# First routing of a mixture-of-experts layer: gates, dummy products and the first silu product reordered

## The chip, the cores and the metric

One core of one Trainium2 chip. The metric is the device time in microseconds of one execution, as the median of several runs. A core has TensorE (PE, matrix products), VectorE (DVE), ScalarE (ACT), GpSimd (POOL) and SyncE (SP), each with its own instruction queue worked off in order; semaphores order them against each other. Here SyncE issues the plain DMAs and the DMA transpositions, GpSimd the gathers and scatters by index.

## The reference

```python
# x [2, 1024, 256], ctx [2, 77, 256], mask [2, 1024, 77]
def xattn(q, k, v, mask, Wq, Wk, Wv, Wo, bo):        # 16 heads of 64
    dots = where(mask, -max, heads(q @ Wq) . heads(k @ Wk) * 64 ** -0.5)
    return merge(softmax(dots) . heads(v @ Wv)) @ Wo + bo
def ffn(x):                                           # 9 experts of 704, top 2
    scores = sigmoid(x @ gate.T + bias)
    top, selected = top_k(scores, 2); top = top / (sum(top) + 1e-20)
    for e in range(9):
        h = silu(x @ w1[e].T) * (x @ w3[e].T)
        out += weight_of(e) * (h @ w2[e].T)
x = x + xattn(layernorm(x), ctx, ctx, mask, ...)
x = x + ffn(layernorm(x), ...)
```

## The kernel before

**Attention.** The 2048 tokens are 16 tiles of 128 (NT = 16), worked in a software pipeline `step(n)` written out by hand for each engine. For tile n TensorE makes the scores; with lags of 2 to 5 steps it turns the probabilities (`prob_turn`), multiplies them by the folded value and output weights (`project`), VectorE adds the residual (`residual`), takes mean and variance (`stats`, `aggregate`), GpSimd the inverse root (`rstd`), VectorE or ScalarE the second layer norm (`normalise2`), TensorE transposes this in fp32 (`gate_turn`), ScalarE copies it (`gate_copy`), TensorE multiplies by the gate (`gate_logits`), VectorE adds the bias (`logits`) and finds the two best experts (`pick`). SyncE stores the normed rows (`store_xn2`), from which GpSimd gathers later.

**Routing in two parts.** The tokens of the first 11 tiles (K1 = 11) are routed first, in the `drain()` between attention and experts, and fill the first 14 expert tiles (NF1). VectorE makes one-hot tables (`experts_of`), TensorE counts (`ranks`), VectorE computes each token's slot (`first_slots`) and the two halves of a one-hot map (`first_rows`, L1323, `v1_ok`), TensorE multiplies them into a list of token ids (`first_ids`, 22 products of 14 columns), VectorE writes the list (`first_index`, `idx_ok`), and GpSimd starts the gathers. `ids_of(0)` gives the expert number of each tile. The rest is routed between the expert tiles.

**Experts.** 40 tiles of 128 gathered tokens (NF). For tile t: GpSimd `gather(t)`, ScalarE and VectorE split it into fp16 high and low parts (`fx_high`, `fx_low`), SyncE transposes by DMA (`turn_tokens`), except tile 0, which TensorE transposes itself (`first_turn`, then `first_high` and `first_low`). TensorE `up(t)`: four groups of six products, the first two for silu, the other two for the factor; ScalarE `silu`, VectorE `hidden`, ScalarE `h_high`, VectorE `h_low`, SyncE transposes by DMA (`turn_hidden`), TensorE `down(t)` with lag 2, ScalarE `weigh`, GpSimd `scatter`. `between(s)` runs in the middle of `up(s)`, behind its second group. Each engine walks the same `fstep(n)`, n from -3.

**Weights.** Expert weights come as 36 chunks of 544 KB through three buffers: SyncE `load_w(c)`, ScalarE `w_high` or `w_direct`, then the low half by GpSimd (`w_low`, up to chunk 30) or VectorE (`w_rest`, chunks 31 to 35). Each low half raises `w_lo_ok` by one, and the load into a buffer waits for the chunk that was in it (L418: `at_least(sp, w_lo_ok, c - SLOTS + 1)`, with SLOTS = 3). At the end of its drain SyncE has, in this order: store_x1(14), store_xn2(13), load_w(34), load_w(35); the first entry of fstep that moves data is turn_tokens(1) at n = -1.

**Dummy products.** `warm(n, bank)` issues n products of 128 x 128 ones into an unused bank. The drain has three places: WARM_IDS ahead of first_ids, WARM_OUT ahead of project(15), WARM_X0 ahead of first_turn.

**Order in the drain.** TensorE, from prob_turn(15): gate_turn(12), WARM_IDS, first_ids, gate_logits(12), WARM_OUT, project(15) with gate_turn(13) ahead of its chunk 4 and WARM_X0, first_turn ahead of chunk 9, then gate_logits(13). VectorE, from experts_of(0): sums(15), residual(13), p_low(14), stats(13), aggregate(13), first_slots, logits(11), first_rows, residual(14), first_index, p_low(15), ids_of(0), normalise2(13), logits(12), stats(14), aggregate(14), w_rest(31), w_rest(32), first_low, logits(13); then in fstep fx_low(1), residual(15), stats, aggregate, normalise2(14); fx_low(2), normalise2(15), shares(0), hidden(0), first_values, logits(14), pick(11). The helper `link` makes VectorE wait for its own last result.

Of the kernel before, what the change touches and what calls it, by code (L numbers as in the profile page):

```python
# [21 lines left out]
ALU = mybir.AluOpType  # L22
# [3 lines left out]
P = 128  # L26
# [11 lines left out]
E9 = 9  # L38
# [32 lines left out]
def build(nc, x, ctxT, mask, wq, wk, wv, wo, bo, wt, gate, gbias, consts, out):  # L71
    with ExitStack() as ctx:
# [221 lines left out]
        W_PRE = 4  # L294
        WARM, WARM_IDS, WARM_OUT, WARM_X0 = 30, 30, 16, 10

# [222 lines left out]
        def _(pe):  # L519
# [118 lines left out]
            def project(i):  # L638
                b = i // TPB
                at_least(pe, x1_ok, i)  # L640
                for c in range(NCH):
                    if i == NT - 1 and c == G_AT:
                        gate_turn(NT - 3)
                    if i == NT - 1 and c == X0_AT:
                        warm(WARM_X0, WARM_LATE)
                        first_turn()
                        eids[0] = expert(0)
                    if c % 4 == 0:
                        pe.wait_ge(pl_ok, 3 * i + c // 4 + 1)
                    for n, (lhs, rhs) in enumerate(((pt_h, b_hi), (pt_l, b_hi), (pt_h, b_lo))):  # L650
                        mm = pe.matmul(ps[:, 6, 0:D], lhs[:, c, :], rhs[:, b, c, :],  # L651
                                       start=(c == 0 and n == 0), stop=(c == NCH - 1 and n == 2))
                mm.then_inc(out_mm, 1)
# [31 lines left out]
            def first_ids():  # L685

                for q in range(2 * K1):
                    pe.wait_ge(v1_ok, q // K1 + 1)
                    mm = pe.matmul(map_of(0)[0], vhot1[:, q, :], R["u1"][:, q // K1, q % K1, 0, :],
                                   start=(q == 0), stop=(q == 2 * K1 - 1))  # L690
# [74 lines left out]
            def drain():  # L765
# [6 lines left out]
                prob_turn(NT - 1)  # L772
                gate_turn(NT + 1 - LAG_G)
                pe.wait_ge(sub_ok, 3 * NT)
                warm(WARM_IDS, WARM_LATE)
                first_ids()
                gate_logits(NT + 1 - LAG_G)
                warm(WARM_OUT, WARM_LATE)
                project(NT - 1)
                gate_logits(NT - 3)  # L780

# [66 lines left out]
            def between(s):  # L848
                if s in (1, 2):
                    gate_logits(NT - 3 + s)  # L850
# [4 lines left out]
            for s in range(NF + 2):  # L855
# [7 lines left out]
                if s < 2:  # L863
                    gate_turn(NT - 2 + s)
                if s == 1:
                    first_weights()
                if s == 2:
                    pe.wait_ge(lg_ok, NT)
# [11 lines left out]
        def _(act):  # L880
# [158 lines left out]
            p_high(NT - 1)  # L1039
            gate_copy(NT + 1 - LAG_G)  # L1040
            sigmoids(0, K1)
            act.activation(mx[:, 0, 0:1], eps[:], ACT.Silu)
            gate_copy(NT - 3)
            first_high()

# [74 lines left out]
        def _(dve):  # L1120
# [142 lines left out]
            def experts_of(ph):  # L1263
# [5 lines left out]
                dve.wait_ge(top_ok, hi)  # L1269
                for k in range(2):  # L1270
                    ins = dve.tensor_tensor(oh[:, k], by_expert(con[:, C_IOTA:C_IOTA + E9], n),
                                            idx[:, k].unsqueeze(2).to_broadcast([P, n, E9]), ALU.is_equal)
                link(ins)
                dve.tensor_tensor(s16[:, 0:hi, :], r["oh"][:, 0, 0:hi], r["oh"][:, 1, 0:hi], ALU.add).then_inc(s16_ok, 1)
# [175 lines left out]
            def drain():  # L1450
# [7 lines left out]
                p_low(NT - 2)  # L1458
                stats(NT - 3)
                aggregate(NT - 3)  # L1460
                first_slots()
                logits(NT - LAG_G)
                first_rows()
                residual(NT - 2)
                first_index()
                p_low(NT - 1)
                ids_of(0)
                normalise2(NT - 3)
                logits(NT + 1 - LAG_G)
                stats(NT - 2)  # L1470
                aggregate(NT - 2)
                w_rest(4 * EARLY + 3)
                w_rest(4 * E9 - 4)
                first_low()
                logits(NT - 3)

# [64 lines left out]
            def fstep(n):  # L1541
                if n == T_END + 1:
                    for g in range(2):
                        end_low(g)
                    return
                if onf(n, 1):
                    h_low(n - 1)
                if onf(n, -2) and n > -2:
                    fx_low(n + 2)
                if n == -1:  # L1550
                    residual(NT - 1)
                    stats(NT - 1)
                    aggregate(NT - 1)
                    normalise2(NT - 2)
                if n == 0:
                    normalise2(NT - 1)
                    shares(0)
                if n == 1:
                    held_of(0)
                if n == 2:  # L1560
# [31 lines left out]
                if n == 12:  # L1592
                    tile_weights(1)
                if onf(n, 0):
                    hidden(n)
                if n == 0:
                    first_values()
                    logits(NT - 2)
                    pick(NT - LAG_G)
                if n == 1:  # L1600
                    pick(NT + 1 - LAG_G)
# [14 lines left out]
        def _(pool):  # L1616
# [49 lines left out]
            def step(n):  # L1666
# [15 lines left out]
                if n == NT - 1:  # L1682
                    w_low(4 * EARLY + 2)
                if on(n, LAG_X1):
                    rstd(n - LAG_X1)
# [40 lines left out]
            def fstep(n):  # L1726
# [6 lines left out]
                if n + 3 == NF1:  # L1733
                    pool.wait_ge(idx_ok, 2)
                    stored(pool, NT - 2)
                    stored(pool, NT - 1)
                if n == -1:
                    rstd(NT - 2)
                if onf(n, -3):
# [59 lines left out]
```

## Time and profile before

| what | value |
|---|---|
| time, median of 3 runs | 423.49 us (422.23 to 424.11) |
| profiled execution | 422.82 us |
| its span | 421.0 us |
| PE busy | 403.9 us (96%), 3176 products |
| DVE, ACT, POOL busy | 275.2, 253.2, 246.9 us |
| L824, products of `up` | 960, 150.1 us |
| L844, products of `down` | 681, 80.8 us |
| mean granted clock of TensorE | 0.989 |

The span runs from the first to the last instruction of the execution; the time has 1.82 us more around it. Times of rows count from the span's start. The attention phase fills the span to about 170 us, the drain and the first expert tiles stand at 170 to 205, and the expert tiles follow to 412.

### The profile page before, as it was taken

The numbers are of one execution on the slowest core, as the hardware profiler recorded it, in microseconds if no ns is written. First come the engines' busy times: TensorE is split into PE (matmuls) and PEld (weight loads), VectorE is DVE, ScalarE is ACT, GpSimd is POOL, SyncE is SP. The second block draws the span as 40 slices with busy tenths as digits, with TensorE's granted clock in tenths as the row PEclk, the third lists the DMA queues.
The fourth block names the chain that finished last, engine by engine and source line by source line (L and its number), as shares of the span: only waits on it lengthen the run. The fifth ranks groups of instructions, "written<-read, shape, count | busy, mean of one in ns | idle before, by whom it ended". The sixth has DMA issues, their size and how long they took to land.

```text
span 421.0 us, 10140 instructions
## 1 busy us (share of the span) xinstructions
PE 403.9 (96%) x3176; PEld 307.2 (73%) x3176; DVE 275.2 (65%) x683; ACT 253.2 (60%) x444; POOL 246.9 (59%) x214
## 2 busy tenths in 40 slices
PE   8999999999999999789899999999999999999991
PEld 7777677778877877776677777777777777777781
DVE  1777989999899988987889854444444444444430
ACT  3759899999999986724655444444444444444430
POOL 6536789998999888253245534445444444444232
PEclk9999999999999999989999999999999999999997
DMA  7994456576575666256789978989889989989742
GB/s 228 342 321 132 132 160 201 161 189 201 155 235 166 177 187 190 74 151 120 154 138 139 146 131 133 141 139 129 150 141 142 141 139 140 143 134 153 119 68 36
DMA packets 106512, 66.03 MB, mean 157 GB/s; under 512 B 80992, under 2 KB 99808, under 8 KB 106464
## 3 DMA queue, kind: packets, MB, share of 16 engines
q1 hardware_dynamic: 98784, 54.90, 57.4%
q0 software_dynamic: 7680, 10.49, 16.5%
q8 instruction: 30, 0.49, 0.5%
q14 instruction: 18, 0.15, 0.1%
HBM read 36.23 MB, written 9.96 MB: 110 GB/s over the span
## 4 chain that ended last, share of the span: by engine, by line
PE 56%; issue 16%; DMA 14%; DVE 4%; POOLq 4%; POOL 3%; SPq 1%; ACT 0%; DVEq 0%
PE ps L824 12%; PE ps L621 12%; PE ps L651 11%; DMA out_rows<-work,idx_all 9%; PE ps L844 7%; PE ps L634 4%; POOLq L1709 3%; PE ps L558 3%; POOL work L1700 3%; PE ps L617 2%; DMA w_all<-in_wv 2%; PE ps L523 1%; DMA work<-work 1%; PE ps L667 1%; DMA work<-xn_rows,idx_all 1%
## 5 line engine op out<-in xcount | busy, mean ns | idle before, releaser
L824 PE MATMUL ps<-w_all,work 128*128 x960 | 150.1, 313 | 0.8 <-DVE work L1447 0.5
L824 PEld LDWEIGHTS ps<-w_all,work 128*128 128x128 f16 x960 | 93.6, 98 | 47.0 <-issue 1.2
L1721 POOL DMA_INDIRECT out_rows<-work,idx_all x40 | 64.2, 1606 | 102.5 <-ACT work L1076 101.1
L1516 DVE SCALAR_TENSOR_TENSOR work<-ps,work 128x352 f32<-128x352 f32 x80 | 41.2, 523 | 66.4 <-PE ps L824 66.3
L844 PE MATMUL ps<-w_all,work 128*128 x681 | 80.8, 273 | 1.1 <-DMA work<-work 1.1
L844 PEld LDWEIGHTS ps<-w_all,work 128*128 128x128 f16 x681 | 66.3, 98 | 12.0 <-issue 1.6
L1641 POOL TENSOR_TENSOR w_all<-stage,w_all 128x1088 f16<-128x1088 f32 x31 | 69.9, 2256 | 6.5 <-ACT w_all L916 6.2
L1055 ACT ACTIVATE work<-ps 128x352 f32<-128x352 f32 x80 | 36.8, 463 | 53.6 <-PE ps L824 53.6
L1061 ACT ACTIVATE work<-work 128x704 f16<-128x704 f32 x39 | 30.8, 790 | 62.2 <-DVE work L1516 62.2
L1700 POOL DMA_INDIRECT work<-xn_rows,idx_all x40 | 40.6, 1014 | 29.9 <-issue 10.3
L621 PE MATMUL ps<-w_all 128*128 128x462 f16 (+1 forms) x288 | 57.4, 336 | 0.0
L651 PE MATMUL ps<-w_all,work 128*128 128x256 f16 x320 | 53.9, 274 | 1.3 <-DVE work L1196 1.3
L621 PEld LDWEIGHTS ps<-w_all 128*128 128x128 f16 x288 | 27.9, 97 | 22.0
L651 PE MATMUL ps<-work 128*128 128x256 f16 x160 | 43.8, 274 | 0.0
L1646 POOL TENSOR_TENSOR work<-work 128x1232 f32<-128x1232 f32 x16 | 36.0, 2250 | 2.9 <-DVE work L1191 2.9
L914 ACT ACTIVATE stage<-stage 128x1088 f32<-128x1088 f32 x31 | 34.5, 1113 | 2.4 <-DMA stage<-in_wt 2.4
L651 PEld LDWEIGHTS ps<-w_all,work 128*128 128x128 f16 x320 | 31.5, 99 | 5.1 <-DVE work L1206 1.4
L916 ACT ACTIVATE w_all<-stage 128x1088 f16<-128x1088 f32 x31 | 34.4, 1111 | 1.0
L1523 DVE TENSOR_TENSOR work<-work 128x640 f16<-128x640 f32 x39 | 31.9, 818 | 0.0
L1522 DVE TENSOR_TENSOR work<-work 128x64 f16<-128x64 f32 x39 | 8.8, 227 | 31.0 <-ACT work L1061 30.9
L1174 DVE TENSOR_REDUCE work<-ps 128x6 f32<-128x462 f32 (+1 forms) x48 | 25.3, 576 | 1.1 <-PE ps L621 1.0
L1187 DVE TENSOR_REDUCE work<-work 128x16 f32<-128x1232 f32 x16 | 22.8, 1423 | 4.6 <-ACT work L937 4.6
(159 smaller groups left out, 537.2 us busy)
## 6 DMA issues: line engine op xcount, KB each, us to landing
stage<-in_wt SPq DMA_DIRECT2D x36, 544.0 KB, 4.4
work<-in_x SPq DMA_DIRECT2D x30, 128.0 KB, 3.7
out_rows<-work SPq DMA_DIRECT2D x18, 128.0 KB, 4.3
xn_rows<-work SPq DMA_DIRECT2D x18, 128.0 KB, 4.1
w_all<-in_x SPq DMA_DIRECT2D x1, 1536.0 KB, 14.6
work<-work SPq DMA_TRANSPOSE x78, 3.6
w_all<-in_wq SPq DMA_DIRECT2D x4, 256.0 KB, 6.8
w_all<-in_wv SPq DMA_DIRECT2D x2, 512.0 KB, 8.2
```

The source lines that it names most:

```text
L621: mm = pe.matmul(dst, lhs[:, par, k, :], rhs[:, k, b, h0 * J:h0 * J + w], start=False, stop=(k == KD - 1 and rhs is a_lo))
L651: mm = pe.matmul(ps[:, 6, 0:D], lhs[:, c, :], rhs[:, b, c, :], start=(c == 0 and n == 0), stop=(c == NCH - 1 and n == 2))
L824: mm = pe.matmul(ps[:, c, 0:half], xt[:, t % 2, block, :], weights(wbase + off, half), start=(k == 0 and n == 0), stop=(k == KD - 1 and n ...
L844: mm = pe.matmul(ps[:, Y_BANKS[t % 2], 0:D], lhs, weights(wbase + (pl * WC + W13C + c * D), D), start=(c == 0 and n == 0), stop=(c == HC - ...
L914: act.activation(stage[:, c % SLOTS, :], stage[:, c % SLOTS, :], ACT.Copy, scale=SP_W).then_inc(w_sc_ok, 1)
L916: act.activation(w_chunk(c, 0), stage[:, c % SLOTS, :], ACT.Copy).then_inc(w_hi_ok, 1)
L1055: act.activation(sg[:, t % 2, c * HID // 2:(c + 1) * HID // 2], ps[:, c, 0:HID // 2], ACT.Silu, scale=1.0 / SP_W).then_inc(silu_ok, 1)
L1516: dve.scalar_tensor_tensor(out=sg[:, t % 2, cols], in0=ps[:, 2 + c, 0:HID // 2], scalar=1.0 / SP_W, in1=sg[:, t % 2, cols], op0=ALU.mult, ...
L1641: pool.tensor_tensor(w_chunk(c, 1), stage[:, c % SLOTS, :], w_chunk(c, 0), ALU.subtract).then_inc(w_lo_ok, 1)
L1646: pool.tensor_tensor(e3, e3, rr[:, i % 2].unsqueeze(2).to_broadcast([P, HEADS, J]), ALU.mult).then_inc(norm_ok, 1)
L1700: pool.indirect_dma_start(out=xg[:, t % 2], out_offset=None, in_=xn2_rows[0:K1 * P, :] if t < NF1 else xn2_rows, in_offset=bass.IndirectOf ...
L1721: pool.indirect_dma_start(out=acc, out_offset=bass.IndirectOffsetOnAxis(ap=idx_all[:, t:t + 1], axis=0), in_=yb[:, t % 2], in_offset=None, ...
```

## The change

On TensorE gate_turn(12) goes from ahead of the first dummies to behind first_ids, gate_logits(12) from there into project(15), gate_turn(13) from there to behind project(15), and gate_logits(13) into the middle of up(0). The dummies become 28, 6 and 4 (they were 30, 16 and 10), with 18 new ones between the two halves of first_ids. first_weights goes from behind up(1) to behind up(2). On VectorE stats(13) and aggregate(13) go from ahead of first_slots to behind ids_of(0), with stats(14) and aggregate(14) next to them; logits(11) goes behind residual(14); normalise2(13) behind w_rest(31); logits(13) behind normalise2(14); w_rest(32) and hidden(0) together to the beginning of fstep(0), ahead of fx_low(2) and normalise2(15); logits(14) and shares(0) to behind h_low(0); first_values, held_of(0) and pick(11) behind hidden(1). The two comparisons of experts_of become one. ScalarE's gate_copy(12) goes behind the sigmoids and the table load for silu, and first_high ahead of gate_copy(13). GpSimd's rstd(13) goes from its last step to fstep(-1), behind gather(1). SyncE's code is unchanged.

```diff
--- before.py
+++ after.py
@@ -292,7 +292,7 @@
         LAG_OUT, LAG_X1, LAG_XN2, LAG_G = 2, 3, 4, 5
         W_STEP = 2
         W_PRE = 4
-        WARM, WARM_IDS, WARM_OUT, WARM_X0 = 30, 30, 16, 10
+        WARM, WARM_IDS, WARM_HALF, WARM_OUT, WARM_X0 = 30, 28, 18, 6, 4
 
         def on(s, lag):
             return 0 <= s - lag < NT
@@ -640,7 +640,7 @@
                 at_least(pe, x1_ok, i)
                 for c in range(NCH):
                     if i == NT - 1 and c == G_AT:
-                        gate_turn(NT - 3)
+                        gate_logits(NT + 1 - LAG_G)
                     if i == NT - 1 and c == X0_AT:
                         warm(WARM_X0, WARM_LATE)
                         first_turn()
@@ -685,6 +685,8 @@
             def first_ids():
 
                 for q in range(2 * K1):
+                    if q == K1:
+                        warm(WARM_HALF, WARM_LATE)
                     pe.wait_ge(v1_ok, q // K1 + 1)
                     mm = pe.matmul(map_of(0)[0], vhot1[:, q, :], R["u1"][:, q // K1, q % K1, 0, :],
                                    start=(q == 0), stop=(q == 2 * K1 - 1))
@@ -770,14 +772,13 @@
                 project(NT - 2)
                 gate_logits(NT - LAG_G)
                 prob_turn(NT - 1)
-                gate_turn(NT + 1 - LAG_G)
                 pe.wait_ge(sub_ok, 3 * NT)
                 warm(WARM_IDS, WARM_LATE)
                 first_ids()
-                gate_logits(NT + 1 - LAG_G)
+                gate_turn(NT + 1 - LAG_G)
                 warm(WARM_OUT, WARM_LATE)
                 project(NT - 1)
-                gate_logits(NT - 3)
+                gate_turn(NT - 3)
 
             for m in range(5):
                 keys(m)
@@ -846,7 +847,7 @@
                 mm.then_inc(w2_mm, 1)
 
             def between(s):
-                if s in (1, 2):
+                if s in (0, 1, 2):
                     gate_logits(NT - 3 + s)
                 if s + 1 < NF:
                     eids[s + 1] = expert(s + 1)
@@ -862,9 +863,8 @@
                     up(s, eids[s] * (2 * WC), lambda: between(s))
                 if s < 2:
                     gate_turn(NT - 2 + s)
-                if s == 1:
+                if s == 2:
                     first_weights()
-                if s == 2:
                     pe.wait_ge(lg_ok, NT)
                 if s == 3:
                     ranks(1)
@@ -1037,11 +1037,11 @@
             w_direct(4 * EARLY + 3)
             w_direct(4 * E9 - 4)
             p_high(NT - 1)
-            gate_copy(NT + 1 - LAG_G)
             sigmoids(0, K1)
             act.activation(mx[:, 0, 0:1], eps[:], ACT.Silu)
+            gate_copy(NT + 1 - LAG_G)
+            first_high()
             gate_copy(NT - 3)
-            first_high()
 
             def fx_high(t):
                 turned(act, t - 2)
@@ -1267,10 +1267,8 @@
                 oh, s16 = r["oh"][:, :, lo:hi], r["s16a"] if ph == 0 else r["s16b"]
                 idx = top_idx[:, 0:2 * NT].rearrange("p (i k) -> p k i", k=2)[:, :, lo:hi]
                 dve.wait_ge(top_ok, hi)
-                for k in range(2):
-                    ins = dve.tensor_tensor(oh[:, k], by_expert(con[:, C_IOTA:C_IOTA + E9], n),
-                                            idx[:, k].unsqueeze(2).to_broadcast([P, n, E9]), ALU.is_equal)
-                link(ins)
+                link(dve.tensor_tensor(oh, by_expert(con[:, C_IOTA:C_IOTA + E9], n).unsqueeze(1).to_broadcast([P, 2, n, E9]),
+                                       idx.unsqueeze(3).to_broadcast([P, 2, n, E9]), ALU.is_equal))
                 dve.tensor_tensor(s16[:, 0:hi, :], r["oh"][:, 0, 0:hi], r["oh"][:, 1, 0:hi], ALU.add).then_inc(s16_ok, 1)
 
             def tiles_of(total):
@@ -1456,23 +1454,21 @@
                 sums(NT - 1)
                 residual(NT - 3)
                 p_low(NT - 2)
-                stats(NT - 3)
-                aggregate(NT - 3)
                 first_slots()
-                logits(NT - LAG_G)
                 first_rows()
                 residual(NT - 2)
+                logits(NT - LAG_G)
                 first_index()
                 p_low(NT - 1)
                 ids_of(0)
-                normalise2(NT - 3)
-                logits(NT + 1 - LAG_G)
+                stats(NT - 3)
+                aggregate(NT - 3)
                 stats(NT - 2)
                 aggregate(NT - 2)
+                logits(NT + 1 - LAG_G)
                 w_rest(4 * EARLY + 3)
-                w_rest(4 * E9 - 4)
+                normalise2(NT - 3)
                 first_low()
-                logits(NT - 3)
 
             a_low(0)
             dve.wait_ge(xall_in[0], 16)
@@ -1543,8 +1539,14 @@
                     for g in range(2):
                         end_low(g)
                     return
+                if n == 0:
+                    w_rest(4 * E9 - 4)
+                    hidden(0)
                 if onf(n, 1):
                     h_low(n - 1)
+                if n == 1:
+                    logits(NT - 2)
+                    shares(0)
                 if onf(n, -2) and n > -2:
                     fx_low(n + 2)
                 if n == -1:
@@ -1552,11 +1554,9 @@
                     stats(NT - 1)
                     aggregate(NT - 1)
                     normalise2(NT - 2)
+                    logits(NT - 3)
                 if n == 0:
                     normalise2(NT - 1)
-                    shares(0)
-                if n == 1:
-                    held_of(0)
                 if n == 2:
                     logits(NT - 1)
                     pick(NT - 3)
@@ -1591,13 +1591,12 @@
                     held_of(1)
                 if n == 12:
                     tile_weights(1)
-                if onf(n, 0):
+                if onf(n, 0) and n > 0:
                     hidden(n)
-                if n == 0:
+                if n == 1:
                     first_values()
-                    logits(NT - 2)
+                    held_of(0)
                     pick(NT - LAG_G)
-                if n == 1:
                     pick(NT + 1 - LAG_G)
                 if n == 2:
                     pick(NT - 1)
@@ -1681,7 +1680,7 @@
                     w_low(w_at(n))
                 if n == NT - 1:
                     w_low(4 * EARLY + 2)
-                if on(n, LAG_X1):
+                if on(n, LAG_X1) and n < NT:
                     rstd(n - LAG_X1)
 
             for n in range(NT + 1):
@@ -1735,6 +1734,7 @@
                     stored(pool, NT - 2)
                     stored(pool, NT - 1)
                 if n == -1:
+                    rstd(NT - 3)
                     rstd(NT - 2)
                 if onf(n, -3):
                     gather(n + 3)
```

## Rows read from the trace of the kernel before

**Rows 1.** Busy by stretch: window, us, PE, PEld, DVE, ACT, POOL, clock, DMA share, GB/s.

```profile
180.00:190.00 10.00, 9.45 (x81) 8.10 (x81) 7.84 (x20) 1.54 (x4) 6.71 (x7) 0.83 0.58 173
...
200.00:202.00 2.00, 1.22 (x9) 0.59 (x6) 1.86 (x12) 2.00 (x4) 0.38 (x1) 1.00 0.89 218
...
240.00:300.00 60.00, 60.00 (x479) 44.64 (x478) 27.98 (x66) 25.73 (x54) 28.96 (x22) 1.00 0.90 138
```

**Rows 2.** The chain that ended last, 178 to 203: start, us, what.

```profile
182.34 1.85 PE ps L651 x12
...
184.41 1.64 PE ps L651 x15
...
192.24 0.41 DVE work L1223
...
197.32 4.74 DMA work<-work
```

**Rows 3.** Instructions of VectorE in order of time: start, us, what, idle before.

```profile
167.28 0.43 DVE L1271 TENSOR_TENSOR work<-con 128x99 f32<-128x99 f32 x2
...
171.43 0.42 DVE L1211 BATCH_NORM_STATS2 work<-work 128x6 f32<-128x256 f32 x1
...
171.98 0.14 DVE L1311 CAST work<-ps 128x9 int32<-128x9 f32 x1
...
175.14 0.17 DVE L1228 TENSOR_TENSOR lg<-ps,gb_b 128x9 f32<-128x9 f32 x1
...
179.94 0.17 DVE L1328 TENSOR_SCALAR idx_all<-ps 128x14 uint32<-128x14 f32 x1 [0.20 <-PE ps L689]
...
183.25 2.60 DVE L1245 SCALAR_TENSOR_TENSOR w_all<-stage,w_all 128x1088 f16<-128x1088 f32 x2
187.29 0.42 DVE L1447 TENSOR_TENSOR work<-ps,work 128x256 f16<-128x256 f32 x1 [1.43 <-ACT work L1006]
```

**Rows 4.** Products of TensorE in order of time.

```profile
175.72 1.84 PE L596 MATMUL ps<-onesb 128*128 128x128 bf16 x30
...
179.46 0.44 PE L689 MATMUL ps<-work,w_all 128*128 128x14 f16 x11 [1.10 <-DVE w_all L1303]
...
180.47 1.87 PE L596 MATMUL ps<-onesb 128*128 128x128 bf16 x16
...
188.06 3.75 PE L824 MATMUL ps<-w_all,work 128*128 x24 [0.55 <-DVE work L1447]
...
192.06 1.96 PE L824 MATMUL ps<-w_all,work 128*128 x12
...
202.30 2.03 PE L844 MATMUL ps<-w_all,work 128*128 x17 [1.08 <-DMA work<-work]
```

**Rows 5.** Instructions of GpSimd in order of time.

```profile
180.41 1.24 POOL L1700 DMA_INDIRECT work<-xn_rows,idx_all  x1 [7.35 <-DVE idx_all L1328]
...
183.43 1.15 POOL L1651 TENSOR_TENSOR work<-work,eps 128x1 f32<-128x1 f32 x1 [0.50 <-DVE work L1217]
184.66 1.64 POOL L1656 TENSOR_TENSOR work<-work,mhalf 128x1 f32<-128x1 f32 x1
...
189.60 0.57 POOL L1656 TENSOR_TENSOR work<-work,mhalf 128x1 f32<-128x1 f32 x1
```

**Rows 6.** Waits of SyncE's queue: who waited for whom: us in total, times, longest.

```profile
SPq L419 <- DVE w_all L1245: 2.5, 2, 1.5
```

**Rows 7.** DMAs issued by SyncE in order of time.

```profile
184.56 1.66 SPq L419 DMA_DIRECT2D stage<-in_wt  x2
188.21 1.28 SPq L493 DMA_TRANSPOSE work<-work  x1
```

**Rows 8.** Issue to landing, 164 to 216: transpositions L493, loads L419, gathers L1700.

```profile
DMA to landing us min/median/max: 2.4/3.1/4.1
...
DMA to landing us min/median/max: 3.7/3.7/5.1
...
DMA to landing us min/median/max: 2.9/3.1/4.0
```

## The prediction

> **What bounds the kernel now.** I read the busy times by stretch first. From 240 us on TensorE is busy in every microsecond [rows 1], so the expert phase runs at TensorE's pace and whatever moves its beginning moves the end one for one. Between the attention phase and that steady part it isn't full: 1.22 of 2.00 us in 200 to 202. The same rows give 180 to 190 a mean granted clock of 0.83; with 1.2 and 2.4 GHz as the only levels that is 3.4 us at half clock. It lies at the front of these ten: 16 dummy products from 180.47 took 1.87 us where 30 took 1.84 at 175.72 [rows 4].
>
> The chain of waits says what ended last there [rows 2]: half-clock products of the last projection (12 in 1.85 us, then 15 in 1.64 at full clock), normalise2(15) on VectorE (192.24), which with shares(0) stands ahead of the first product hidden(0), and the transposition of the first hidden tile, 4.74 us from 197.32. Down(0), the first second-layer product, began at 202.30 after an idle 1.08 us [rows 4]. After it TensorE has no gap. I therefore use one number as the mark: the start of down(0). The profiled execution took 422.82 us, 1.82 more than its span of 421.0; the median of the runs is 423.49, 0.67 above it.
>
> **Part 1, the ids.** Statistics and aggregation of tile 13 left from ahead of first_slots: its first instruction stood at 171.98, the statistics at 171.43, so 0.55. Logits(11) goes from between first_slots and first_rows: at most its 0.17, at least 0 as such short ones overlap; I take 0.1. Merging the two comparisons saves between 0 and half of their 0.43; I take 0.07, nearer to nothing as the elements stay. Sum 0.7 [rows 3]. Everything behind waits on VectorE alone, so first_index goes from 179.94 to 179.2. The 28 dummies (30 took 1.84) begin 0.3 earlier, as gate_turn(12) is gone from ahead of them and the softmax is 0.07 earlier, and end at 177.1; the first half of first_ids follows at 177.2; 18 dummies of 0.06 take 1.1 of the 1.3 us until the second half is allowed at 178.75. The idle 1.10 before the second half [rows 4] becomes about 0.1. The clock fell just behind that idle time and narrow products; with dense ones in it I expect full clock. That gives back 16 dummies at 1.87 against 0.98, 12 products at 1.85 against 1.31 [rows 2, 4] and some 0.25 on the gate products between: 1.7.
>
> **Part 2, up to the first expert product.** From first_index to first_turn TensorE took 6.7 us (179.94 to 186.61: 15 products from 184.41 end at 186.05, 10 dummies of 0.06 follow; rows 2, 3). Off go 1.7 of clock and 16 dummies at full rate (10 of WARM_OUT, 6 of WARM_X0), 0.95. Gate_turn(12) and gate_logits(12) stay on this stretch and gate_turn(13) leaves it: level. Project(15) now waits some 0.3 for p_low(15), which the dummies had covered. So 179.2 + 4.3 = 183.5 for first_turn. Its gather lands 2.9 to 4.0 us after issue [rows 8]; issued 0.47 behind first_index (180.41 on GpSimd, rows 5), now 179.7, it's there between 182.6 and 183.7: no wait, at worst 0.2.
>
> First_low needs VectorE too. Its queue from ids_of: both pairs of statistics and aggregation (0.55 each) end at 182.7, logits(12) 0.1, w_rest(31) 1.3 (two took 2.60, rows 3) to 184.1, then normalise2(13). This one waits for rstd(13), which GpSimd did long before in the old order and now does behind two gathers, while w_rest runs. The two GpSimd instructions that ran beside w_rest took 1.15 and 1.64 us and ended when it did or just behind it, the same power took 0.57 with VectorE free [rows 5]. So rstd(13) ends at 184.5, 0.4 behind w_rest(31), normalise2(13) at 184.9, first_low follows, and up(0) starts 0.77 behind first_low's start (187.29 to 188.06, rows 3, 4): 185.7 against 188.06, **2.4 us earlier**.
>
> The Trainium skill (SBUF — State Buffer, Who interferes with whom) says that a VectorE instruction with two SBUF inputs and a GpSimd instruction that reads SBUF exclude each other, for the whole of the one that starts first. The trace agrees, as far as the 1.15 and 1.64 go. Without that lock rstd(13) would be hidden under w_rest and up(0) would start at 185.2; with GpSimd first, w_rest would wait, to much the same end as mine.
>
> **Part 3, what SyncE waits for.** Here I expect the change to lose. SyncE's queue ends the drain with store_xn2(13), load_w(34), load_w(35), and only then comes turn_tokens(1), the transposition that up(1) needs. Load_w(35) refills the buffer of chunk 32 and waits for 33 weight chunks done, that is for w_rest(32). In the kernel before w_rest(32) runs inside the drain: SyncE waited for the two w_rest 2.5 us in all, issued the loads by 186, and turn_tokens(1) at 188.21 was held by nothing but fx_low(1) [rows 3, 6, 7]. The change moves w_rest(32) behind residual(15), statistics, normalise2(14) and logits(13), and logits(13) waits for gate_logits(13), which now sits in the middle of up(0). Half of up(0) is 1.8 us (188.06 to 191.64 whole), the gate's four products and the hand-over to VectorE I estimate at 0.6, from the 0.77 of the hand-over between first_low and up(0): 185.7 + 1.8 + 0.6 = 188.1. W_rest(32) takes 1.3 to 189.4, the load goes out, the transposition at 189.8. Not held it could have gone at 186.5, behind fx_low(1) (first_low ends at 185.3, and ScalarE's gate copy and fx_high(1), 0.4 each by the like of L1447, lie between).
>
> Its landing: such transpositions took 2.4 to 4.1 us, a 544 KB load 3.7 to 5.1 [rows 8], and now the load stands directly ahead of it on the same queue. Bounds 2.4 and 5.1, I take 4.1, above the middle because of the load: up(1) starts at 193.9, between 192.2 and 194.9. Before it was 192.06. TensorE is through with up(0), gate_logits(13) and gate_turn(14) at 189.9 and stands idle for 4 us.
>
> **Part 4, from up(1) to down(0).** Before: 202.30 - 192.06 = 10.24, of which 1.08 waited for the hidden tile and 0.18 for hidden(0). The products stay the same (first_weights only passes behind up(2)), so 9.0. Hidden(0) no longer stands behind normalise2(15) and shares(0): it ends at 190.5, its transposition goes out near 194 behind SyncE's stores and lands at 198.7 with the slow 4.74, before TensorE arrives at 202.9. What is late next is VectorE: pick(11) and pick(12) now stand ahead of h_low(1), logits(15) comes some 9.1 behind up(1), and down(0) waits for it: 0.1, at most 0.5. So down(0) at 193.9 + 9.1 = 203.0, 0.7 late: -2.4 at up(0), +4.2 at the wait, -1.1 of idle time covered.
>
> **Part 5, the clock.** A pause of 4 us without a product is longer than any in rows 1 and 4. The pause of 1.1 with narrow products around it was followed by 3.3 us at 0.50. Half clock over up(1) costs half of the part that falls on products: 0 to 1.7 us; as some of the low stretch can lie in the pause I take 1.4. The Trainium skill (TensorE: Matmul & The Clock Gate, HAM oscillation) describes exactly this, products that wait for a DMA and find the clock halved. No row of this trace has so long a pause.
>
> **Sum**: 0.7 + 1.4 = 2.1 us later: 422.82 + 2.1 = 424.9 against the profiled execution, 425.6 against the median. I say 425.2.
>
> **Rivals.**
> *The wait on SyncE costs nothing (faster).* Were load_w(35) released before 187, transposition and up(0) would end together at 190.4, down(0) would start at 190.4 + 9.0 = 199.4, 2.9 earlier: 420.0 to 420.6. It decides from the point where turn_tokens(1) lands before 190. For it: all the rest of the change gains, and the waits of rows 4 are hit squarely by the new dummies. Against it: SyncE's wait for w_rest stands in rows 6, and its order is unchanged.
> *Held, but the clock stays up*: only the 0.7, 423.5 to 424.2. For it: the 1.08 idle at 201 passed at full clock.
> *The clock falls in the drain all the same*, since the ids remain 22 narrow products: up(0) and what follows some 1.2 later, 426.5 or so. For it: the kernel before had 30 dummies there and fell.
> *VectorE becomes the bound in the first expert tiles* (w_rest(32), shares(0) and four picks have moved between its products): another 1 to 2 us, 427. Against it: VectorE is 1.86 of 2.00 us busy in 200 to 202 but only 27.98 of 60 later [rows 1], so it can catch up.
>
> **How the numbers follow.** Held with half clock 0.45, held at full clock 0.20, not held 0.17, clock down in the drain 0.12, VectorE 0.06. The likeliest alone has 423.8 to 427; with the bounds and the faster case 420.5 to 428. No change is within 2.1 us of 423.49, about what a measurement can tell: 421.4 to 425.6. Faster: most of the third case, 0.16. Same: the second and nearly half of the first, 0.43. Slower: the rest, 0.41.
>
> **What would show it.** First_index near 179.2 and full clock around 180 (parts 1, 2); up(0) near 185.7; SyncE's load_w(35) behind w_rest(32) at 189.4 and its transposition right behind; TensorE idle some 4 us ahead of up(1), then 0.50 for a while; down(0) with no wait on a transposition, near 203 to 204.5. A transposition issued before 187.5 makes the prediction wrong, and so does a full TensorE between up(0) and up(1).

## The result, and the profile after

The changed kernel took 427.47 us (median of 6, 426.54 to 427.85); the kernel before 422.84 (median of 6, 422.23 to 424.11). The ratio is 1.0103, 95% interval 1.0085 to 1.0121: 3.6 to 5.1 us slower. Forecast were 425.2, with 420.5 to 428. The profiled execution took 426.54, the fastest of the six, and 3.72 more than the one of before.

The page of the changed kernel, its first lines:

```profile
span 424.7 us, 10138 instructions
## 1 busy us (share of the span) xinstructions
PE 404.6 (95%) x3176; PEld 306.5 (72%) x3176; DVE 275.0 (65%) x681; ACT 253.3 (60%) x444; POOL 247.4 (58%) x214
```

TensorE's products after, in order of time (start, us, what, idle before), against [rows 4]:

```profile
177.21 1.17 PE L596 MATMUL ps<-onesb 128*128 128x128 bf16 x18
178.45 0.43 PE L691 MATMUL ps<-work,w_all 128*128 128x14 f16 x11
...
183.91 0.44 PE L747 MATMUL ps<-con,work 128*128 128x128 f32 x2 [0.37 <-DMA work<-xn_rows,idx_all]
...
185.47 1.96 PE L825 MATMUL ps<-w_all,work 128*128 x12
...
194.94 3.33 PE L825 MATMUL ps<-w_all,work 128*128 x12 [5.14 <-issue]
...
205.05 2.03 PE L845 MATMUL ps<-w_all,work 128*128 x17
...
211.53 0.24 PE L678 MATMUL ps<-work,trib 128*128 128x153 bf16 x1 [0.84 <-DVE work L1272]
```

The new dummies fill the idle 1.10 of [rows 4], and up(0) starts 2.59 us earlier (185.47 against 188.06). Then TensorE stands for 5.14 us, and the first twelve products of up(1) take 3.33 us where others take 1.96. Down(0) starts 2.75 us late, and a second wait follows, 0.84 ahead of ranks(1).

The part ahead of all this doesn't last equally long in two executions: VectorE's first instruction of the drain stands between 166.21 and 167.43 us in the fourteen traces of this document. In the trace of before and in that of after:

```profile
167.20 0.07 DVE L1453 MEMSET work<- 128x9 bf16 x1
```

```profile
166.69 0.07 DVE L1451 MEMSET work<- 128x9 bf16 x1
```

Reckoned from it, up(0) is 2.08 early (18.78 against 20.86), up(1) 3.39 late, down(0) 3.26 late, and the end 4.2 late (258.0 against 253.8). That agrees with the 4.4 of the ratio, and the table below gives all traces that way. Of the six executions the profiled one has, with one other, the highest mean granted clock (0.990; the four from 427.25 to 427.85 us have 0.987 or 0.988), so the trace shows a mild case.

SyncE's queue after (instructions, then its waits), against [rows 6, 7]:

```profile
184.39 5.27 SPq L419 DMA_DIRECT2D stage<-in_wt  x2
189.78 1.28 SPq L493 DMA_TRANSPOSE work<-work  x1
```

```profile
SPq L419 <- DVE w_all L1245: 4.5, 1, 4.5
```

The two loads stand as one group of 5.27 us because the second waited 4.5 for w_rest(32). The transposition for up(1) follows it.

VectorE and GpSimd after, in order of time, against [rows 3, 5]:

```profile
178.93 0.17 DVE L1326 TENSOR_SCALAR idx_all<-ps 128x14 uint32<-128x14 f32 x1
...
182.39 1.28 DVE L1245 SCALAR_TENSOR_TENSOR w_all<-stage,w_all 128x1088 f16<-128x1088 f32 x1
183.59 0.41 DVE L1223 TENSOR_SCALAR work<-work 128x256 f32<-128x256 f32 x1
184.79 0.42 DVE L1445 TENSOR_TENSOR work<-ps,work 128x256 f16<-128x256 f32 x1 [0.80 <-ACT work L1006]
...
187.94 0.16 DVE L1228 TENSOR_TENSOR lg<-ps,gb_b 128x9 f32<-128x9 f32 x1
188.01 1.28 DVE L1245 SCALAR_TENSOR_TENSOR w_all<-stage,w_all 128x1088 f16<-128x1088 f32 x1
189.21 1.00 DVE L1512 SCALAR_TENSOR_TENSOR work<-ps,work 128x352 f32<-128x352 f32 x2
```

```profile
182.25 0.58 POOL L1655 TENSOR_TENSOR work<-work,mhalf 128x1 f32<-128x1 f32 x1
182.81 0.91 POOL L1650 TENSOR_TENSOR work<-work,eps 128x1 f32<-128x1 f32 x1
```

W_rest(32) (the second L1245) ends at 189.3, directly behind logits(13). The power of rstd(13) began before w_rest(31), took its usual 0.58, and w_rest(31) its usual 1.28: normalise2(13) (L1223) waited for nothing.

TensorE by stretch after (columns as in rows 1; the clock is third from the right):

```profile
178.00:182.00 4.00, 3.71 (x47) 3.14 (x45) 3.78 (x13) 1.32 (x3) 2.23 (x3) 1.00 0.23 68
190.00:194.00 4.00, 0.00 (x0) 0.00 (x0) 1.98 (x5) 1.01 (x2) 2.48 (x2) 1.00 0.95 221
195.00:197.00 2.00, 2.00 (x8) 1.01 (x9) 0.00 (x0) 0.32 (x2) 0.00 (x0) 0.50 0.84 189
```

The half clock moved from the drain to up(1): full in 178 to 182, no product at all in 190 to 194, then 0.50.

### The profile page after: what moved, and what is told of

The parts are those of the page before. It is cut to its first block, busy times and chain, and to the rows that moved or that the text cites. A ratio compares the mean times of both kernels' runs of the same rounds, so it can differ in the third digit from the quotient of the medians.

```text
span 424.7 us, 10138 instructions
## 1 busy us (share of the span) xinstructions
PE 404.6 (95%) x3176; PEld 306.5 (72%) x3176; DVE 275.0 (65%) x681; ACT 253.3 (60%) x444; POOL 247.4 (58%) x214
## 4 chain that ended last, share of the span: by engine, by line
PE 58%; issue 17%; DMA 12%; DVE 4%; POOLq 4%; POOL 3%; ACT 1%; SPq 0%; DVEq 0%; ACTq 0%
PE ps L825 14%; PE ps L621 12%; PE ps L651 10%; DMA out_rows<-work,idx_all 9%; PE ps L845 6%; PE ps L634 4%; POOLq L1708 3%; PE ps L558 3%; POOL work L1699 3%; PE ps L617 2%; PE ps L523 2%; DMA w_all<-in_wk 1%; PE ps L535 1%; PE ps L667 1%; DMA work<-xn_rows,idx_all 1%
## 5 line engine op out<-in xcount | busy, mean ns | idle before, releaser
L1699 POOL DMA_INDIRECT work<-xn_rows,idx_all x40 | 41.6, 1041 | 33.8 <-DVE work L1505 11.8
```

Source lines behind the costliest of these rows:

```text
L1699: pool.indirect_dma_start(out=xg[:, t % 2], out_offset=None, in_=xn2_rows[0:K1 * P, :] if t < NF1 else xn2_rows, in_offset=bass.IndirectOf ...
```

## The experiments

Each was timed beside the kernel before, whose medians there were 422.87 to 423.16 us; ratios are to those, with their 95% intervals. The medians are of 4 to 12 executions. The last four columns are from each one's profile: start of up(0), up(1), down(0) and the end of the span, all less the start of VectorE's first instruction of the drain.

| kernel | us, median | ratio (interval) | up(0) | up(1) | down(0) | end |
|---|---|---|---|---|---|---|
| before | 422.84 | 1 | 20.9 | 24.9 | 35.1 | 253.8 |
| changed | 427.47 | 1.0103 (1.0085 to 1.0121) | 18.8 | 28.2 | 38.4 | 258.0 |
| e1_load_behind | 421.79 | 0.9971 (0.9952 to 0.9989) | 19.2 | 23.4 | 33.1 | 253.0 |
| e2_pause_filled | 425.95 | 1.0074 (1.0045 to 1.0102) | 18.7 | 28.2 | 37.0 | 256.6 |
| e3_w_rest_alone | 428.02 | 1.0108 (1.0061 to 1.0155) | 20.8 | 29.2 | 40.4 | 259.1 |
| e5_no_half_dummies | 421.88 | 0.9978 (0.9960 to 0.9996) | 18.4 | 24.6 | 33.3 | 252.9 |
| e4_load_and_ranks | 420.40 | 0.9942 (0.9927 to 0.9957) | 18.5 | 22.7 | 32.3 | 250.9 |
| e6_w_rest_in_drain | 422.84 | 0.9996 (0.9978 to 1.0013) | 19.1 | 26.0 | 34.7 | 254.6 |
| e7_ranks_behind | 426.01 | 1.0069 (1.0050 to 1.0088) | 19.0 | 28.4 | 38.7 | 257.5 |
| e8_load_not_ahead | 424.25 | 1.0030 (1.0017 to 1.0043) | 18.8 | 25.4 | 35.7 | 255.5 |
| e9_silu_first | 421.00 | 0.9959 (0.9945 to 0.9973) | 19.0 | 23.2 | 33.1 | 251.4 |
| e10_half_dummies_alone | 423.40 | 1.0012 (0.9995 to 1.0029) | 19.7 | 25.1 | 35.5 | 254.3 |
| e11_before_load_behind | 421.66 | 0.9979 (0.9962 to 0.9996) | 20.8 | 24.6 | 34.9 | 253.4 |
| e12_before_load_and_dummies | 421.25 | 0.9953 (0.9937 to 0.9969) | 19.6 | 23.4 | 33.8 | 252.5 |

**Does the load hold the transposition?**

```diff
-            load_w(4 * E9 - 1)          # end of SyncE's drain
                 if n == -1:
                     store_x1(NT - 1)
                     store_xn2(NT - 2)
+                    load_w(4 * E9 - 1)
```

> The changed kernel with SyncE's load_w(35) issued behind turn_tokens(1) and the last stores, instead of ahead of them. Theory (the load's wait for w_rest(32) held the transposition that up(1) needs): turn_tokens(1) is issued near 186.6 in place of 189.78, lands near 190.4, up(1) starts at 190.5 in place of 194.94, the half clock over its first twelve products (1.4 us) goes as well, and down(0) starts near 199.5 in place of 205.05; some 5 us off the changed kernel's 427.5, so 421.5 to 423, at or below the kernel before. Rival (the transposition is late for another reason, the gathers or the moved gates): at most 1 us off, 426.5 or more.

SyncE, then TensorE of e1_load_behind, in order of time:

```profile
187.65 1.28 SPq L492 DMA_TRANSPOSE work<-work  x1
```

```profile
186.36 1.96 PE L825 MATMUL ps<-w_all,work 128*128 x12
...
190.52 1.95 PE L825 MATMUL ps<-w_all,work 128*128 x12
...
200.24 2.03 PE L845 MATMUL ps<-w_all,work 128*128 x17
...
206.79 0.24 PE L678 MATMUL ps<-work,trib 128*128 128x153 bf16 x1 [0.91 <-DVE work L1272]
```

Up(1) starts at 190.52 with no idle time, down(0) at 200.24. One load in another place takes away 5.7 us of medians; the theory holds, its rival falls. The transposition itself went out at 187.65 and not at 186.6: in this execution the first gather came late (first_turn waited 0.79 for it) and all behind it with it. It was then used 2.87 us after its issue.

**Is it the moved w_rest(32) by itself?** The kernel before with `w_rest(4 * E9 - 4)` taken from the drain to the head of fstep(0):

> The kernel before with one edit: w_rest(32) leaves the drain and stands at the start of fstep(0), behind normalise2(14). Theory: load_w(35) and with it turn_tokens(1) are held until w_rest(32) ends near 190.8 and the transposition lands near 195.5 in place of 191.9; up(1) is 3 to 3.5 us later, half clock may add 1, the wait for the first hidden tile is covered by 1: 2 to 4 us slower than before, 425 to 427. Rival (w_rest(32) alone is harmless, and it is logits(13) waiting for the gate in the middle of up(0) that does it): less than 1 us slower.

SyncE and TensorE of e3_w_rest_alone:

```profile
184.49 6.52 SPq L419 DMA_DIRECT2D stage<-in_wt  x2
191.12 1.28 SPq L493 DMA_TRANSPOSE work<-work  x1
```

```profile
196.35 3.70 PE L824 MATMUL ps<-w_all,work 128*128 x12 [4.45 <-issue]
```

A like pause (4.45 us), half clock behind it, and a ratio of 1.0108: by the intervals this one move costs about as much as the whole change. Here logits(13) stood in its old place, so the rival (the gate in the middle of up(0)) isn't needed. The time is 1 us above what was expected, and the interval is wide. The clock is a reason: three of the four executions have a mean granted clock of 0.981 and took 428.01 to 428.85 us, the fourth has 0.989 and took 425.40. In the profiled one (0.981) the half clock lasted into the second twelve products of up(1):

```profile
200.56 2.45 PE L824 MATMUL ps<-w_all,work 128*128 x12
```

The other remedy, `w_rest(4 * E9 - 4)` behind normalise2(13) in the drain of the changed kernel:

> The changed kernel with w_rest(32) back in the drain, between normalise2(13) and first_low, where VectorE idled 0.80 us. SyncE's order stays. Theory: w_rest(32) ends near 185.2, load_w(35) goes out then, turn_tokens(1) follows fx_low(1) at 186.8; first_low is at most 0.5 later; up(1) near 191; 4.5 to 5.5 us below the changed kernel, 422 to 423. Rival (only the order on SyncE helps): 424.5 or more.

```profile
187.08 1.28 SPq L493 DMA_TRANSPOSE work<-work  x1
```

```profile
193.33 1.96 PE L825 MATMUL ps<-w_all,work 128*128 x12 [2.58 <-issue]
```

The time is in the expected range, but not for the expected reason alone. The transposition went out at 187.08 as foreseen, and up(1) began only at 193.33, 6.25 us later, where I had expected 191. The rival, that only SyncE's order helps (424.5 or more), falls by the median.

**How slow is a transposition behind a load?** The changed kernel with

```diff
+                if n == -1:
+                    sp.wait_ge(w_lo_ok, 4 * E9 - 3)
                 if onf(n, -2) and n > -2:
                     turn_tokens(n + 2)
+                if n == -1:
+                    load_w(4 * E9 - 1)
```

> The changed kernel, but turn_tokens(1) itself waits for w_rest(32) and the load of chunk 35 comes right behind it on the same queue. The transposition goes out at the same moment as in the changed kernel, near 189.4, with no fresh 544 KB load ahead of it. Theory (the load ahead made the landing 5.0 instead of some 3.5 us): lands near 192.8, up(1) starts about 1.7 earlier, 425.5 to 426.2. Rival (the 5.0 is made by the gathers and by what else moves then): landing still 4.5 or more, only the 0.4 of the load's issue gone, 427 or more.

```profile
190.06 1.28 SPq L492 DMA_TRANSPOSE work<-work  x1
```

```profile
192.75 3.06 PE L828 MATMUL ps<-w_all,work 128*128 x12 [2.27 <-issue]
```

Issued 190.06, used at 192.75: 2.7 us against 5.2 in the changed kernel (189.78 to 194.94), for a transposition that goes out only 0.4 sooner, reckoned from the drain (22.7 against 23.1). The theory's direction holds; its 3.5 us for the landing was too long, so the gain (3.1 us by the ratios) is larger than expected.

**The clock.** 84 dummies (`warm(84, X0_BANK)` behind gate_turn(14)) in the pause:

> The changed kernel with 84 dummy products into an unused bank between gate_turn(14) and up(1), some 4.7 us at full clock, inside the pause of 5.1. They compute nothing. Theory: the pause stays, since the wait is for a transposition, but the clock doesn't fall and the first twelve products of up(1) take 1.96 us in place of 3.33; 1.2 to 1.5 us off, near 426.1. Rival (the 1.4 us in those products isn't the clock but the operands or the DMAs landing beside them): no change, 427.5.

```profile
190.31 4.86 PE L596 MATMUL ps<-onesb 128*128 128x128 bf16 x84
195.66 1.96 PE L825 MATMUL ps<-w_all,work 128*128 x12 [0.48 <-issue]
```

The transposition came no sooner (issued at 190.44 in this trace, used at 195.66), and the twelve products took 1.96 us again. 1.2 us off by the ratios, 1.5 by the medians. The intervals of the two kernels overlap, so the times alone don't show it; the table has 1.4 us at down(0) and at the end, and the mean granted clock was 0.995 or 0.996 in all four executions, against 0.987 to 0.990 in the six of the changed kernel. The half clock is that part of the loss.

e1_load_behind with WARM_HALF = 0:

> As e1_load_behind, but without the 18 dummy products between the two halves of first_ids. Theory: TensorE idles 1.1 us there again, the clock falls near 180 for some 3.4 us, up(0) starts about 1 us later than in e1_load_behind, and the kernel takes 0.8 to 1.5 us more. Rival (moving gate_turn(12) and the dummies ahead was enough, the clock stays up): the same time as e1_load_behind within 0.3.

TensorE of e5_no_half_dummies, then its stretch 178 to 182:

```profile
178.63 0.43 PE L691 MATMUL ps<-work,w_all 128*128 128x14 f16 x11 [1.10 <-DVE w_all L1301]
```

```profile
178.00:182.00 4.00, 3.16 (x38) 2.79 (x39) 3.77 (x13) 1.49 (x3) 2.11 (x2) 1.00 0.20 59
```

The idle 1.10 is back, the clock is full all the same in this profile, and the median is that of e1_load_behind: the rival wins. But not in every execution. Seven of the ten have a mean granted clock of 0.993 or 0.994 and took 421.22 to 422.36 us; three have 0.989 or 0.990 and took 422.83 to 423.54. With the dummies (e1_load_behind) none of ten is below 0.992. So they may still prevent a fall in some executions; where in those three the clock fell isn't known, as they have no trace. (Up(1) waits 1.89 here for a transposition issued 1.4 us behind load_w(34).)

The kernel before with only those 18 dummies:

> The kernel before with one edit: 18 dummy products between the two halves of first_ids, where TensorE idled 1.10 us. Theory of the prediction: the clock no longer falls near 180 and 1.5 to 1.7 us are saved up to first_turn; the start of up(0) then waits for w_rest and first_low as before, so 0.8 to 1.5 us off the 423.1. Rival, from e5_no_half_dummies, where the clock stayed up without them: the fall depends on the execution and on the order behind the ids, and the dummies change less than 0.5 us.

```profile
186.95 1.29 SPq L493 DMA_TRANSPOSE work<-work  x1
```

```profile
186.71 3.75 PE L826 MATMUL ps<-w_all,work 128*128 x24 [0.45 <-DVE work L1449]
...
192.14 1.96 PE L826 MATMUL ps<-w_all,work 128*128 x12 [1.47 <-issue]
```

The clock stays up in this profile, and up(0) starts 1.2 earlier by the table. Then up(1) waits 1.47 for its transposition and starts no sooner than before (25.1 against 24.9). The time doesn't move. The theory was right on the profile's clock and wrong on what it is worth; the rival has the time right, and its "depends on the execution" is partly so: the kernel before has no dummies there, and of its 21 executions beside e4_load_and_ranks eight have a mean granted clock of 0.995 or 0.996. They took 422.40 to 424.26 us, no less than the five at 0.990 (422.00 to 423.52). What a full clock gains there is lost again ahead of up(1), which the two loads ahead of its transposition, unchanged from before, hold up.

**The second wait.** e1_load_behind, and the changed kernel itself, with `ranks(1)` behind `down(1)` on TensorE:

> e1_load_behind, and TensorE's ranks(1) behind down(1) instead of ahead of it. In the trace of e1_load_behind TensorE stood 0.91 us ahead of ranks(1), for VectorE's experts_of(1), which ends 0.9 late. Theory (this second wait lies on the path): 0.8 to 0.9 us less than e1_load_behind, near 420.9, and 1.9 to 2.1 below the kernel before. Rival (what the wait covered comes up elsewhere, VectorE's later tiles or the counts behind the ranks): no more than 0.3 less.

> The changed kernel with only ranks(1) behind down(1); load_w(35) stays ahead of turn_tokens(1). Theory: the 0.84 us that TensorE stood ahead of ranks(1) goes, 426.6 in place of 427.5; with the pause ahead of up(1) and its half clock these three are the whole loss. Rival: no change, since VectorE has been late by as much for the next tile.

TensorE of e4_load_and_ranks:

```profile
189.45 1.96 PE L825 MATMUL ps<-w_all,work 128*128 x12
...
194.59 1.96 PE L825 MATMUL ps<-w_all,work 128*128 x12 [0.80 <-ACT work L1055]
...
204.57 2.02 PE L845 MATMUL ps<-w_all,work 128*128 x17
206.42 0.23 PE L678 MATMUL ps<-work,trib 128*128 128x153 bf16 x1
```

The wait is gone in both: 1.2 us from 0.9971 to 0.9942, and 1.4 from 1.0103 to 1.0069. Both are somewhat more than the 0.91 and 0.84 of the traces; the intervals allow these too. It lay on the path, and the way from down(0) to the end says so without any interval: 219.6 to 219.9 us in the six traces that have the wait, 218.3 to 218.8 in the eight that haven't, the kernel before (218.7) among them.

The 0.80 ahead of up(2), silu(1) put ahead of fx_high(3):

> e4_load_and_ranks, and on ScalarE silu(1) ahead of fx_high(3) instead of behind it. In the trace of e4_load_and_ranks up(2) waited 0.80 us for silu(1), which stood behind fx_high(3) and its gather. Theory: that wait goes, 0.6 to 0.8 us less, near 419.7. Rival (the next tile's transposition comes 0.8 later for it and takes the wait over, as fx_high(3) is then behind silu(1)): no change.

```profile
194.94 1.96 PE L825 MATMUL ps<-w_all,work 128*128 x12 [0.32 <-issue]
...
200.16 2.03 PE L845 MATMUL ps<-w_all,work 128*128 x17 [0.56 <-DVE lg L1228]
```

The wait halves and another, down(0) on the last logits, takes its place: not the one that the rival had named. No gain (0.9959 against 0.9942), though this execution also waited 0.64 for its first gather and has up(0) 0.5 later than that of e4_load_and_ranks.

**What is the rest of the change worth?** The kernel before with the load behind, alone and with the 18 dummies:

> The kernel before with only load_w(35) behind turn_tokens(1) and the stores. Theory (in the kernel before too, the transposition lands late because loads stand ahead of it, but down(0) is bound by the first hidden tile behind normalise2(15) and shares(0)): turn_tokens(1) lands about 1 us earlier, down(0) hardly moves; 0 to 0.6 off the 423.1. Rival (the load order alone is the whole gain of e1_load_behind, and the rest of the change is worth nothing): 421.8, as e1_load_behind.

> The kernel before with the 18 dummy products between the halves of first_ids (e10_half_dummies_alone) and load_w(35) behind turn_tokens(1). In e10_half_dummies_alone up(0) came 1.35 us earlier and up(1) gave it back waiting for its transposition. Theory: with the load out of the way up(1) keeps 1 to 1.35 of it, and down(0) as much less its own wait for the first hidden tile; 0.5 to 1.3 us off the 423.1. Rival (the first hidden tile's transposition binds down(0) at 202.3 to 202.6 whatever comes ahead): under 0.3.

TensorE of e11_before_load_behind:

```profile
190.78 1.95 PE L824 MATMUL ps<-w_all,work 128*128 x12
...
201.08 2.03 PE L844 MATMUL ps<-w_all,work 128*128 x17 [1.06 <-DMA work<-work]
```

The load behind alone gives 0.9979, and e1_load_behind with the whole change in it 0.9971. By the intervals these two aren't told apart, and both forecasts of e11_before_load_behind stay possible (0.2 to 1.6 us off). Its trace speaks for the theory: up(1), down(0) and the end only 0.2 to 0.4 sooner than before, with down(0) still waiting 1.06 for the hidden tile, and a drain that began 1 us early, ahead of anything that the edit touches. With the dummies too, up(0) comes 1.2 sooner and, the transposition being in time now, up(1), down(0) and the end keep it (1.4, 1.3 and 1.3), 0.9953 by the times: a bit more than the theory's range, and against its rival. The dummies are worth something only once the load is out of the way. The best kernel measured is e4_load_and_ranks, 0.9942, 2.4 us under the kernel before.

## Why the prediction was right or wrong

**Part 1, the ids.** First_index stood at 178.93 (forecast 179.2), but the drain had begun 0.51 early; reckoned from it the gain is 0.50 for 0.7, so the better number is luck. The idle 1.10 is gone, and the clock was full in 178 to 182. Not shown is the cause, which I gave to the dummies in the pause: without them the clock stayed up as well in the profile of e5_no_half_dummies, and seven of its ten executions are as fast as with them. In the old order it fell in the drain in the profiles of the kernel before, e3_w_rest_alone and e11_before_load_behind and not in the two with the dummies; what else in the new order keeps it up I haven't separated.

**Part 2, up to up(0).** 185.47 against 185.7, but half a microsecond of that is the early drain; reckoned from the drain the gain is 2.1 for 2.4. The inner steps were less good: I took 6.7 us from first_index to first_turn before the change, where the trace has 6.5 (first_turn at 186.44 and not 186.61); after it, first_turn waited 0.37 for its gather (4.45 us from its issue at 179.41, above the bound of 4.0), and the delay of rstd(13) by w_rest(31) didn't come, since both its instructions had started before. The two errors nearly cancelled. The Trainium skill (SBUF — State Buffer, Who interferes with whom) lets whichever of the two instructions starts first block the other. With VectorE first the trace agrees: rstd(14)'s first instruction took 0.91 where others took 0.19 to 0.30. With GpSimd first it doesn't show: in all nine traces of the new order the power of rstd(13) began 0.14 us ahead of w_rest(31) and ran beside it, and w_rest(31) kept its 1.28.

**Part 3, SyncE.** The mechanism, shown by e1_load_behind and e3_w_rest_alone: w_rest(32) ended at 189.3 (189.4) and the transposition went out at 189.78 (189.8). The mis-sized term is its landing: I took 4.1 us and up(1) at 193.9; it took 5.2, up(1) 194.94, at the very edge of the bounds. My bounds came from transpositions with no load close ahead (the one of before was issued 2.3 us behind a load and took 3.7) and from loads by themselves, and no row had the case itself; e8_load_not_ahead shows that the load made the difference (2.7 without it).

**Part 4, to down(0).** 9.1 forecast; measured 10.11 less 1.37 of clock, 8.7. Down(0) met no wait. What I missed is the wait ahead of ranks(1), 0.84. I had VectorE as a rival, with the moved picks among its reasons and 1 to 2 us as its price, and gave it 0.06. The cover that vanished was the 1.08 that down(0) used to wait for the hidden tile: before, VectorE was ready for ranks(1) 5.1 us behind the start of down(0), after 6.4. In e4_load_and_ranks and e7_ranks_behind the wait goes.

**Part 5, the clock.** 1.4 forecast, 1.37 in the profile, 1.2 to 1.5 in e2_pause_filled. In the four executions with the lower mean clock it can be more; they have no trace.

**The sum.** 2.1 forecast, 4.2 in the profiled pair reckoned from the drain, 4.4 by the ratio. Short were the landing (+1.0), the wait ahead of ranks(1) (+0.84), up(0) (+0.3) and the way from up(0) to the transposition (4.31 for 4.1); long was part 4 (-0.4). So the forecast's sum had half of the loss: the path was right, its terms too small, and by its own bound for "no change" (425.6) the result is slower, which had 0.41. The rival "held, but the clock stays up" is refuted by the profile. The rival "costs nothing" is what e1_load_behind builds: forecast 420.0 to 420.6, measured 421.8, short by the wait ahead of ranks(1) and a new one ahead of up(2).

## What to carry to other kernels

Before an instruction is moved later on one engine, list the semaphores it raises and look in every other queue, DMA queues above all, for a wait on them and for what is queued behind that wait: here the refill of a buffer, first read some 22 us later (issued at 189.3, read at 211.39), held the transposition needed next. When a wait is closed, look at what the other engines did in it. And put bulk loads behind a small urgent transfer of the same queue, not ahead: the dummies that saved 1.2 us upstream were worth nothing until that was done.

## What the runs showed of the hardware

A DMA transposition issued close behind 544 KB loads of the same queue came late by far more than its own time. From issue to the product that used it, TensorE waiting: 5.2 us with a load 0.4 to 0.5 us ahead (changed kernel, e2_pause_filled, e3_w_rest_alone), 5.2 and 6.25 with the second of two loads 1.2 ahead (e10_half_dummies_alone, e6_w_rest_in_drain), 5.5 with one load 1.4 ahead (e5_no_half_dummies), and 2.7 with none for 5 us (e8_load_not_ahead). Further ahead the load did little: 2.9 us at most with one 2.1 and 2.8 ahead (e4_load_and_ranks, e1_load_behind), 3.3 to the landing with one 2.5 ahead (e12_before_load_and_dummies), 3.7 with the second of two 2.3 ahead (kernel before). In e5 and e6 the load ahead was slow too, 5.8 and 7.0 us to its landing against 3.6 to 5.1 for the loads issued at 183 to 192 in the other traces; what slowed both there no run separates.

TensorE's clock was full after a pause of 1.10 us with narrow products on both sides in the profile of e5_no_half_dummies, and fell after the same pause in the kernel before [rows 4]: the pause by itself doesn't decide it. It was at half behind the pause in the three profiles with over 4 us without products that no dummies filled (the changed kernel, e3_w_rest_alone, e7_ranks_behind), and some 0.7 us behind the end of one of 2.27 (e8_load_not_ahead), but not behind one of 2.58 (e6_w_rest_in_drain).
